# Value parts copied into packed rows of 132 bytes, and two adjacency tiles staged in the mask buffer

## The reference

```python
# layer 0: graph attention, 8 heads of 64 units
feats  = einsum('bnf,hfu->bhnu', x, W)
e_self, e_neigh = feats . a_self, feats . a_neigh
dense  = leaky_relu(e_self[..., :, None] + e_neigh[..., None, :], 0.2)
dense  = dense - 1e10 * (1 - adj)
out    = einsum('bhij,bhju->bhiu', softmax(dense, -1), feats) + b
x      = layernorm(x + relu(out))
# layer 1: mean over neighbours, then a 1024 -> 512 product
agg    = (adj @ x) / maximum(sum(adj, -1), 1e-6)
x      = layernorm(x + relu(concat([x, agg]) @ W1.T))
```

## Time and profile before

| | us |
|---|---|
| median of 3 runs | 3538.81 (3531.39 to 3540.57) |
| the profiled execution: its time, its span | 3539.05, 3537.1 |
| PE busy | 3394.3 (96%) |
| DVE busy | 2461.7 (70%) |
| ACT busy | 1872.3 (53%) |
| the three groups of value matmuls, 16384 each | 1554.6, 1554.1, 1554.1 |

### The profile page before, as it was taken

One profiled execution on the slowest core, in us unless ns is written; L12 is line 12 of the kernel. 1 busy time (PEld: TensorE's weight loads), 2 busy tenths in 40 slices (PEclk: granted clock), 3 DMA queues, 4 the chain that ended last, 5 costly groups with the idle time before them and its releaser, 6 DMA issues.

```text
span 3537.1 us, 135243 instructions
## 1 busy us (share of the span) xinstructions
PE 3394.3 (96%) x58432; PEld 2886.4 (82%) x58432; DVE 2461.7 (70%) x4364; ACT 1872.3 (53%) x2441; POOL 285.1 (8%) x252
## 2 busy tenths in 40 slices
PE   5999999999999999999999999999999999999998
PEld 4978879787796877968789697896978879788795
DVE  4857668576685766858678585785857758576685
ACT  3736546364464645636456363563736537365463
POOL 0020200202001020010201002010020200202001
PEclk9999999999999999999999999999999999999999
DMA  4113031130311303122031220312203131130310
GB/s 170 52 31 128 27 115 57 36 114 23 115 58 46 107 21 118 54 64 89 23 124 45 75 84 20 127 39 83 77 25 128 33 108 52 31 128 27 96 34 24
DMA packets 98396, 248.37 MB, mean 70 GB/s; under 512 B 14720, under 2 KB 14720, under 8 KB 97792
## 3 DMA queue, kind: packets, MB, share of 16 engines
q1 hardware_dynamic: 97792, 239.38, 20.6%
HBM read 205.26 MB, written 34.08 MB: 68 GB/s over the span
## 4 chain that ended last, share of the span: by engine, by line
PE 82%; DVE 9%; issue 5%; DMA 2%; ACT 2%; SPq 0%; DVEq 0%; ACTq 0%; POOL 0%; POOLq 0%
PE six L859 69%; PE pair L859 9%; DVE xs L738 2%; DVE stats L743 2%; PE six L996 2%; DVE feat L630 1%; DMA out_dram<-mask 1%; PE pair L888 1%; PE six L888 1%; DVE rs L751 0%; PE pair L897 0%; ACT x_parts L472 0%; DVE trl L619 0%; PE six L897 0%; DVE nb L753 0%
## 5 line engine op out<-in xcount | busy, mean ns | idle before, releaser
L859 PE MATMUL six<-rest,mask 128*128 128x65 bf16 x16384 | 1554.6, 194 | 3.1 <-issue 2.6
L859 PE MATMUL six<-x_parts,mask 128*128 128x65 bf16 x16384 | 1554.1, 193 | 2.2 <-issue 0.8
L859 PE MATMUL six<-third,mask 128*128 128x65 bf16 x16384 | 1554.1, 193 | 0.2
L859 PEld LDWEIGHTS six<-x_parts,mask 128*128 128x128 fp8e4 x16384 | 1538.2, 97 | 9.7 <-issue 8.0
L859 PEld LDWEIGHTS six<-rest,mask 128*128 128x128 fp8e4 x16384 | 1534.3, 97 | 6.8 <-issue 4.6
L859 PEld LDWEIGHTS six<-third,mask 128*128 128x128 fp8e4 x16384 | 1537.7, 97 | 0.0
L450 ACT ACTIVATE step<-s_bc,n_step 128x1024 uint16<-128x1024 f32 x1024 | 1092.1, 1138 | 369.7 <-DVE mask L688 369.0
L688 DVE TENSOR_TENSOR mask<-adj_t,step 128x1024 uint16<-128x1024 uint16 x1024 | 651.3, 685 | 24.7 <-ACT step L450 24.7
L859 PE MATMUL six<-adj_t,x_parts 128*128 128x512 fp8e4 x1536 | 387.3, 379 | 8.8 <-ACT x_parts L472 6.4
L393 POOL TENSOR_TENSOR s_bc<-feat,rden 128x512 f32<-128x512 f32 x112 | 124.1, 1113 | 3009.6 <-DVE s_bc L731 2980.8
L859 PEld LDWEIGHTS six<-adj_t,x_parts 128*128 128x128 f16 x1536 | 146.1, 98 | 186.4 <-issue 24.9
(11 more groups left out here) (117 smaller groups left out, 4952.0 us busy)
## 6 DMA issues: line engine op xcount, KB each, us to landing
adj_nat<-in_adj_dram SPq DMA_DIRECT2D x128, 512.0 KB, 4.5
s_bc<-self_scores SPq DMA_DIRECT2D x128, 512.0 KB, 3.8
xs<-in_x_dram SPq DMA_DIRECT2D x128, 256.0 KB, 4.1
out_dram<-mask SPq DMA_DIRECT2D x128, 256.0 KB, 3.9
adj_nat<-in_x_dram SPq DMA_DIRECT2D x64, 256.0 KB, 5.2
step<-in_x_dram SPq DMA_DIRECT2D x64, 256.0 KB, 3.7
xs<-in_L_gnn_W_dram SPq DMA_DIRECT2D x1, 2048.0 KB, 11.7
feat<-in_L_gnn_W_dram SPq DMA_DIRECT2D x4, 256.0 KB, 3.6
```

The source lines that it names most:

```text
L859: return pe.matmul(o, l, r, start=start, stop=stop, skip_group_check=True)
```

## The change

1. The first two parts are also packed. One set of `whole` and `rest` (`val32`, a buffer of its own) serves all heads. ACT copies its upper halves to packed arrays in one pass per head (`pack_head`, 2080 elements per partition), for head 0 in two halves of two copies each (`pack_first_head`, 520 elements each). DVE writes the third part there itself. All three have rows of 66 bf16 (132 bytes), of which 65 are read. Two sets, for even and odd heads, lie in the buffer of `x1_parts`.
2. PE waits for the packed parts, and `value_parts` of the next head for the copy of the one before.
3. The first half of head 0's parts moves ahead of `feature_rows(5)`; a one-element Sigmoid loads ACT's table before the first copy.
4. Adjacency tiles 6 and 7 no longer pass through the three slots. They are loaded to slots 4 to 7 of the mask buffer once the last head's sums are done (for graph 0 at the start), so 3, 4 and 5 are the only late tiles. `degrees` runs in the order 0, 1, 2, 6, 7, 3, 4, 5 and is spread over the output tiles 0 to 7.
5. POOL's `x1_low(1)` waits for the last head's sums, since odd heads' packed parts reach into that tile.

```diff
+    STAGED = 6
+    DEG_ORDER = (0, 1, 2, 6, 7, 3, 4, 5)
+    DEG_AT = {0: (0,), 1: (1,), 2: (2,), 4: (6,), 5: (7,), 6: (3, 4)}
...
-        val32 = [head_of(pool32[:, 0:HEAD]), head_of(pool32[:, T * D - HEAD:T * D])]
-        lower = pool32[:, HEAD:HEAD + HALF_HEAD].rearrange("p (t u) -> p t u", u=U1)
+        U2 = U1 + 1
+        PART = 2 * T * U2
+        packed = [parts_at(0), parts_at(2 * T * D - PARTS * PART)]
+        val = [[words[:, i, :, :, 0:U1] for i in range(PARTS)] for words in packed]
+        val32 = sb("val32", [P, 2, 2, T, U1], F32)
+        lower = sb("lower", [P, T, U1], F32)
...
-        val = [(upper_half(val32[i]), upper_half(rest32[i]), third[:, i]) for i in range(2)]
+        adj_staged = mask32[:, 4 * D:8 * D].rearrange("p (s n) -> p s n", s=T - STAGED)
...
@@ sync, inside the loop
+                sp.wait_ge(sums_ps.sem, sums_ps.at(b, H * GROUPS))
+                for t in range(STAGED, T):
+                    load_adj(b + 1, t)
                 store_scores(b + 1, 0)
                 for t in range(T):
-                    for late in {4: (3, 4), 5: (5, 6), 6: (7,)}.get(t, ()):
+                    for late in {4: (3, 4), 5: (5,)}.get(t, ()):
                         load_late_adj(b + 1, late)
@@ gpsimd
                     pool.wait_ge(x1_ok.sem, x1_ok.at(b, t + 1))
+                    if t == 1:
+                        pool.wait_ge(sums_ps.sem, sums_ps.at(b, H * GROUPS))
@@ scalar, batch
+                def pack_first_head(tiles):
+                    act.wait_ge(val_rest.sem, val_rest.at(b, 1 if tiles.stop == HALF else 2))
+                    for i in range(2):
+                        copy(packed[0][:, i, :, tiles, 0:U1],
+                             upper_halves[:, i, :, tiles]).then_inc(val_packed.sem, 1)
+                def pack_head(h):
+                    act.wait_ge(val_rest.sem, val_rest.at(b, h + 2))
+                    copy(packed[h % 2][:, 0:2]..., upper_halves...).then_inc(val_packed.sem, 1)
...
+                act.activation(warm[:], eps[:, 0:1], ACT.Sigmoid)
+                pack_first_head(FIRST)
                 for g in range(H * T):
                     make_step(g)
+                    if g == 3:
+                        pack_first_head(SECOND)
+                    if g == 10:
+                        pack_head(1)
+                    if g >= 2 * T and g % T == 0:
+                        pack_head(g // T)
...
                     if more and t == T - 1:
+                        degrees(b + 1, 5)
                         act.wait_ge(o2_ps.sem, o2_ps.at(b, T))
@@ vector, value_parts
+                whole, rest = val32[:, 0, :, tiles], val32[:, 1, :, tiles]
+                if h >= 1:
+                    dve.wait_ge(val_packed.sem, val_packed.at(b, h + 3))
+                    dve.wait_ge(val_p2.sem, val_p2.at(b, h + 1))
...
-                dve.tensor_tensor(last, rest, second, ALU.subtract).then_inc(val_p2.sem, 1)
+                dve.tensor_tensor(val[h % 2][2][:, :, tiles], rest, upper_halves[:, 1, :, tiles],
+                                  ALU.subtract).then_inc(val_p2.sem, 1)
@@ vector, batch
-                feature_rows(b, 5)
...
                 value_parts(b, 0, FIRST)
+                feature_rows(b, 5)
@@ tensor, batch
                     pe.wait_ge(val_p2.sem, val_p2.at(b, h + 2 if h else 1))
+                    pe.wait_ge(val_packed.sem, val_packed.at(b, h + 4 if h else 2))
...
                         if h == 0 and jt == HALF:
                             pe.wait_ge(val_p2.sem, val_p2.at(b, 2))
+                            pe.wait_ge(val_packed.sem, val_packed.at(b, 4))
```

More of the change, by code:

```diff
@@ L157, in gat_sage_kernel @@
         degc = sb("degc", [P, T], F32)
+        warm = sb("warm", [P, 1], F32)
         deg_sum = sb("deg_sum", [P, T], F32)
@@ L334, in _ @@
             store_scores(0, 0)
-            for t in range(3, T):
+            for t in range(3, STAGED):
                 load_late_adj(0, t)
@@ L339, in _ @@
                 for s in range(2):
-                    sp.wait_ge(at_ps.sem, at_ps.at(b, T - 1 + s))
+                    sp.wait_ge(at_ps.sem, at_ps.at(b, STAGED - 2 + s))
+                    stand(sp)
                     sp.wait_ge(deg_row.sem, deg_row.at(b, T - 1 + s))
@@ L344, in _ @@
                     load_lead(b + 1, 2 * s + 1)
+                sp.wait_ge(at_ps.sem, at_ps.at(b, STAGED))
+                stand(sp)
                 load_adj(b + 1, 2)
@@ L427, in degrees @@
             def degrees(b, t):
[L428 to L432, removed]
+                done = DEG_ORDER.index(t)
+                adj_landed(act, b, t)
+                if done:
+                    act.wait_ge(deg_row.sem, deg_row.at(b, done))
+                act.activation(row_copy[:], adj_rows_at(t), ACT.Copy,
                                accum_out=deg_sum[:, t:t + 1]).then_inc(deg_row.sem, 1)
@@ L455, in weight_exp @@
                     act.activation(o, a[:], ACT.Exp, scale=k).then_inc(weights.sem, 1)
+                def pack_first_head(tiles):
[5 more added lines that the diff above has]
+                    act.wait_ge(val_rest.sem, val_rest.at(b, h + 2))
+                    copy(packed[h % 2][:, 0:2].rearrange("p s k t u -> p (s k t) u")[:, :, 0:U1],
+                         upper_halves.rearrange("p s k t u -> p (s k t) u")).then_inc(val_packed.sem, 1)
                 score_rows(b, 1)
@@ L528, in batch @@
                         ln1_root(t - 1)
[L529 to L533, removed]
+                    if more and t == 0:
+                        act.wait_ge(rdeg_ok.sem, rdeg_ok.at(b, 1))
+                        act.wait_ge(deg_row.sem, deg_row.at(b, T))
+                    for row in DEG_AT.get(t, ()) if more else ():
+                        degrees(b + 1, row)
                 ln1_root(T - 1)
-                if more:
-                    degrees(b + 1, T - 2)
-                    degrees(b + 1, T - 1)
             for t in range(HALF):
@@ L544, in _ @@
                 x_high(0, t)
-            for t in range(T):
+            for t in DEG_ORDER:
                 degrees(0, t)
@@ L589, in value_parts @@
                 dve.wait_ge(val_f32.sem, val_f32.at(b, count))
-                dve.tensor_tensor(rest, whole, first, ALU.subtract).then_inc(val_rest.sem, 1)
+                dve.tensor_tensor(rest, whole, upper_halves[:, 0, :, tiles], ALU.subtract).then_inc(val_rest.sem, 1)
                 dve.wait_ge(val_rest.sem, val_rest.at(b, count))
-                dve.tensor_tensor(last, rest, second, ALU.subtract).then_inc(val_p2.sem, 1)
+                dve.tensor_tensor(val[h % 2][2][:, :, tiles], rest, upper_halves[:, 1, :, tiles],
+                                  ALU.subtract).then_inc(val_p2.sem, 1)
             def head_sums(b, h, k0, k1):
```

41 lines of the change are left out of this document (22 added, 19 removed).

## The result

The changed kernel takes 3611.1 us (median of 4 runs, 3604.1 to 3615.2) beside 3536.0 of the kernel before on the same chip (3531.4 to 3540.6, 4 runs): ratio 1.0208, 95% interval 1.0194 to 1.0222. It is slower by 75 us. The forecast was 3552 with a range of 3510 to 3582: the sign was right, the size was not, and the time lies outside the range. The profiled execution took 3610.8 us (span 3608.7), 71.6 us of span more than before.

A forecast was written before the change was run, and what follows sets the result against it. PE, working 96% of the span, was taken as the bound. 3539 + 21 (waits less pitch gain, 15 graphs) - 5 (issue stops) - 3 (staged tiles) = 3552 us, range 3510 to 3582.

The forecast's parts named there:

- "issue" stops: PE's stops without a semaphore wait: part of them falls into the new waits, 0.3 us a graph, -5 us.
- The copies: ACT's pass over 2080 elements per head: 1.99 us, about 1.85 in a full queue, between 1.6 and 2.2.
- the pitch: Interval between value matmuls on PE: falls from 31.3 to 30.4 ns with packed rows, gaining 2.8 us a graph.
- head 0: PE waits 0.8 us ahead of tile 4 and 2.0 ahead of tile 7, losing 2.8 us a graph.
- the two signs: The forecast would be wrong if PE has no stop in head 0, or the pitch leaves 30.0 to 31.3 ns.
- Heads 1 to 3: PE waits 1.3 us at tile 29 and 0.1 at tile 21: 1.4 us a graph lost.
- Staged tiles, degrees, prologue: Adjacency loads and degree sums: -3 us once before the loop, nothing inside it.
- The first: Rival: value matmul pitch stays at 31.3 ns, no gain, waits of 3.0 us a graph, 3578 us; chance 0.17.
- The second: Rival: pitch falls to 30.0 ns throughout and waits in heads 0, 2 and 3 grow, 3542 us; chance 0.23.

The follow-up runs named there:

- three mends: The changed kernel with the second half's copies at step 6, 32 bytes of padding ahead of the features and 12 idle VectorE prologue instructions: 3543.1 us, ratio 1.0011.
- TensorE moved: The version with three mends plus 24 idle instructions in TensorE's prologue: 3536.0 us, ratio 0.9985 to the kernel before.
- still less traffic: The changed kernel with score rows of heads 2 to 7, the next graph's first three adjacency loads and leading x tiles cut to 64 columns: 3607.8 us.

## Why the prediction was wrong, point by point

- **What bounds the kernel.** Right: nearly every microsecond is one that PE works or stands. The step that failed is the term for its "issue" stops, counted as a small fixed cost of which waits would absorb 5 us: they cost 40.6 us more. Beside it the sum has no term at all for layer 1, and that measured +36 us. The copies, the pitch and head 0 came out near their forecast, and neither of the two signs by which the forecast was to be found wrong (no stop in head 0, a pitch outside 30.0 to 31.3) came: neither looks at these two.
- **Pitch of the value matmuls.** Forecast 30.4 ns, -44 us; measured 30.18, -56.5. Undersized, and to the kernel's favour. The rule on bf16 strides that the prediction takes from the Trainium skill (SBUF — State Buffer, Door 1: The DMA port swizzle), by which packing gains nothing, did not hold for these matmuls: 1.15 ns each.
- **Head 0.** Forecast waits of 0.8 and 2.0 us ahead of tiles 4 and 7, 2.8 a graph; measured 0.77 and 2.04, 43.1 us. The mechanism is the forecast's own, and moving the copies took it away.
- **Heads 1 to 3.** Forecast 1.3 ahead of tile 29 and 0.1 ahead of tile 21, +21 us. Tile 29 waits 0.28 in 12 graphs; all such waits together cost 8.7. Oversized; which step of the walk through four heads was off, no run shows.
- **Issue stops.** Forecast -5, measured +40.6 inside the tiles. From one place to the next PE has some 125 value matmuls: 3.92 us at 31.33 ns, 3.77 at 30.18. The three kernels at 31.3 to 31.6 ns have 7 to 11 us of stops, the eleven at 30.1 to 30.5 have 31 to 68: the quicker pace goes with more of them. Pitch and stops inside tiles, added per value matmul, are 31.24 ns (changed), 31.29 (rows of 130), 31.52 (three mends), 31.43 (TensorE moved), 31.1 (no copies, with and without the padding) and 30.8 (still less traffic), beside 31.56 before. So of a gain of about 1.15 ns a matmul 0.0 to 0.4 stayed in the kernels that leave nothing out, and up to 0.8 in those that do. The sum is no fixed rate. That the stops are waits for instruction packets is shown, by their shift with the stream and their distance from the landings. What makes the packets late isn't: cutting most of the transfers took two fifths of it at best, and the last graph, whose heads have the same value matmuls, has 0.4 us of such stops in the changed kernel and 2.2 with three mends, beside 2 to 6 in most others. Why is open.
- **Layer 1.** Forecast nothing, measured +36 us, half of the miss and more: 18.8 ahead of `turn_x1(0)`, 14.4 in the intervals of the products behind it, 5.0 the clock there, -2.1 the rest. The two larger parts can't be had from counting operations. One is an address: `val32` and `lower` came to stand ahead of `feat`, 10400 bytes a partition, and moved all that lies behind by 32 bytes against steps of 64; the padding in either kernel shows it, 12 and 17 us. The other is a place in VectorE's instruction stream, shown by the 12 idle instructions.
- **Staged tiles, degrees, prologue.** Forecast 0 and -3; the prologue gave -1.6, and alone this half is at -8.1 us by the medians, -1 to -9 by the interval. The cover was there.
- **Rivals.** The first came closest in time (3578) by luck, since the pitch did fall. The second had the pitch right (30.0, 3542) and lacked layer 1 and the packets.

## What to carry to other kernels

When an engine is busy 95% with short instructions, ask of a quicker instruction whether its code arrives as fast: the stops called "issue" in the profile before are the first sign, and they grow rather than vanish. A pass put ahead in a queue must be walked through to the first consumer of what stands behind it, and moved if that consumer is the bound: here three steps later were worth 36 us. And when a buffer is added, compare the intervals of untouched instructions before and after; 32 bytes or a dozen idle instructions can be worth more than the change.

The version with the staging alone (3531.3 us, 0.9986, 0.9975 to 0.9997) and the one with all mends and TensorE's instructions moved (3536.0, 0.9985, 0.9972 to 0.9997) are the two that compute everything and come out ahead of the kernel before, by 0.03 to 0.3%. That is so little that 24 idle instructions decide it: without them the version with three mends stands at 1.0011. The staging alone is the simpler one to keep.

## What the runs showed of the hardware that I had not expected

- Float32 products of 128x512 start 227 ns apart, or 233 to 234.5, and 32 bytes of padding ahead of the buffers decide which.
- The same VectorE pass takes 0.69 us, or 1.67 if it starts 0.04 us after a GpSimd pass.
- After a stop of 1.9 us in PE's queue the granted clock fell to 0.50 for 3.4 us in some graphs, and a key tile took 2.64 us instead of 1.46.
- A value matmul with 65 moving columns takes 30.15 ns with packed rows of 132 bytes, 30.46 with 130, 31.33 with two of three parts read at a stride of two elements.
- TensorE's instructions come in 16 KB packets, and nine in ten of the stops for one end 1.3 to 1.6 us after it has landed.
